# Linear-attention layer stack: queries held token by token, their denominators on VectorE, the FFN residual first on GpSimd

## The reference

```python
q = _phi((h @ wq + bq_).reshape(b, s, H, DH))        # _phi(t) = elu(t) + 1
k = _phi((h @ wk + bk_).reshape(b, s, H, DH))
v = (h @ wv + bv_).reshape(b, s, H, DH)
kv = jnp.einsum('bshd,bshm->bhdm', k, v)
z = 1.0 / (jnp.einsum('bshd,bhd->bsh', q, k.sum(axis=1)) + 1e-06)
att = jnp.einsum('bshd,bhdm,bsh->bshm', q, kv, z).reshape(b, s, d)
h = h + att @ wo + bo_
h = _ln(h, g1_, be1_)
y = jax.nn.gelu(h @ w1 + c1_, approximate=False) @ w2 + c2_
return (_ln(h + y, g2_, be2_), None)
```

## Time and profile before

| what | us |
| --- | --- |
| median of 3 runs | 918.11 (917.62 to 920.5) |
| the profiled execution | 918.29 |
| its span, first to last instruction | 916.2 |

### The profile page before, as it was taken

How to read it: one execution, slowest core, us unless ns; L and a number is a source line. 1 busy time by engine, 2 the same in 40 slices (tenths; PEclk the granted TensorE clock), 3 DMA queues, 4 the chain that set the end, 5 groups by cost and what they waited for, 6 DMA issues and landing times.

```text
span 916.2 us, 19024 instructions
## 1 busy us (share of the span) xinstructions
PE 877.0 (96%) x5786; PEld 746.0 (81%) x5786; DVE 765.4 (84%) x2737; ACT 705.5 (77%) x1104; POOL 241.2 (26%) x272
## 2 busy tenths in 40 slices
PE   6799999999999999999999999999999999998876
PEld 3588888888888888888888888888888888877664
DVE  7888789787987878788888878878897888899898
ACT  4799887878787887878787788878878787876553
POOL 5222221322232223312232233222223222212103
PEclk9999999999999999999999999999999999999895
DMA  4200100010000100010000100001000000000002
GB/s 130 73 1 17 26 1 22 1 42 1 0 21 0 40 1 20 0 40 0 1 21 0 40 1 19 2 16 25 1 21 0 0 0 1 9 17 1 1 1 92
DMA packets 21888, 16.21 MB, mean 18 GB/s; under 512 B 3920, under 2 KB 17855, under 8 KB 21824
## 3 DMA queue, kind: packets, MB, share of 16 engines
q1 hardware_dynamic: 20960, 14.95, 5.8%
q10 hardware_dynamic: 864, 0.59, 0.2%
HBM read 13.43 MB, written 2.10 MB: 17 GB/s over the span
## 4 chain that ended last, share of the span: by engine, by line
PE 78%; DVE 16%; issue 4%; ACT 1%; DMA 0%; DVEq 0%; ACTq 0%
PE down_ps L753 21%; PE q_ps L703 6%; PE small_ps L692 5%; PE q_ps L685 5%; PE att_ps L722 5%; PE k_ps L679 5%; PE up_ps L747 4%; PE up_ps L745 4%; PE up_ps L746 4%; PE t_ps L729 3%; PE t_ps L669 3%; DVE st L963 2%; PE small_ps L697 2%; PE att_ps L711 1%; PE small_ps L706 1%
## 5 line engine op out<-in xcount | busy, mean ns | idle before, releaser
L753 PEld LDWEIGHTS down_ps<-w_use,hid 128*128 128x128 f32 x2048 | 249.6, 192 | 29.3 <-issue 29.2
L753 PE MATMUL down_ps<-w_use,hid 128*128 128x128 f32 x2048 | 260.4, 275 | 0.0
L1004 POOL TENSOR_TENSOR res_att<-z_tm,g_att 128x512 f32<-128x512 f32 x64 | 81.5, 1273 | 495.9 <-DVE mv L969 495.9
L855 ACT ACTIVATE hid<-up_ps 128x512 f32<-128x512 f32 x192 | 114.9, 599 | 19.9 <-PE up_ps L747 4.3
L963 DVE BATCH_NORM_STATS2 st<-h 128x6 f32<-128x128 f32 x512 | 105.5, 279 | 2.3
L881 ACT ACTIVATE den<-q_ps,den_eps_col 128x512 f32<-128x512 f32 x64 | 43.9, 686 | 59.1 <-PE q_ps L703 59.0
L1011 POOL TENSOR_TENSOR res_ffn<-z_tm,g_ffn 128x512 f32<-128x512 f32 x64 | 81.5, 1273 | 20.7 <-DVE h L958 20.7
L938 ACT ACT_TABLE_LOAD x63 | 80.8, 1283 | 1.1
L745 PE MATMUL up_ps<-z_hi,w_hi 128*128 128x512 f32 x192 | 80.8, 421 | 0.4 <-DVE z_lo L998 0.4
L922 ACT ACT_TABLE_LOAD x62 | 79.5, 1283 | 1.1
L986 DVE TENSOR_SCALAR z_tm<-h,rstd,shift 128x128 f32<-128x128 f32 x256 | 76.3, 360 | 2.3
(11 more groups left out here) (200 smaller groups left out, 1780.1 us busy)
## 6 DMA issues: line engine op xcount, KB each, us to landing
raw_w<-in_L_attn_W SPq DMA_DIRECT2D x15, 256.0 KB, 4.8
out_y<-gate_tm SPq DMA_DIRECT2D x8, 256.0 KB, 2.1
bias_bc<-in_L_attn_c SPq DMA_DIRECT2D x7, 256.0 KB, 4.5
x_tm<-in_L_attn_x SPq DMA_DIRECT2D x3, 512.0 KB, 5.1
raw_g<-in_L_attn_g SPq DMA_DIRECT2D x14, 64.0 KB
x_tm<-in_L_attn_x SPq DMA_DIRECT2D x2, 256.0 KB, 3.2
raw_att<-in_L_attn_Wq SPq DMA_DIRECT2D x7, 64.0 KB, 1.8
raw_att<-in_L_attn_Wk SPq DMA_DIRECT2D x7, 64.0 KB, 1.9
```

The lines of the kernel that those rows point to most:

```text
L753: last = nc.tensor.matmul(down_ps[:, t, :], hid[:, j, t * P:(t + 1) * P], w2_use[:, j, :], start=False, stop=(j == FC - 1 and t == TT - 1))
L855: nc.scalar.activation(hid[:, j, :], up_bank[j], ACT.Gelu).then_inc(s["gelu"], 1)
L1004: nc.gpsimd.tensor_tensor(res_att[:, :, :], z_tm[:, b, :, :], g_att[:, :].unsqueeze(1).to_broadcast([P, TT, D]), ALU.mult).then_inc(s["t2m ...
```

## The change

Queries become token-major. `pe_q` issues four 128-column matmuls with the state as the stationary operand, where it issued one of 512 columns. `q_elu` (one VectorE instruction) takes the place of q_e's and q_phi's two, and leaves out the "+1", which is added where q_elu is read. The key sums now come out of L698's matmul equal on every partition (its operands are swapped), so that VectorE can multiply them with the queries (`dve_q_ks`), sum by head of 8 features (`dve_den`, 64 sums a partition), add the epsilon and take the reciprocal (`dve_rden`, two instructions of 64 elements), and divide (`dve_q_n`). The divided queries are transposed on TensorE (`pe_qn_transpose`, four transposes into the bank of `att_ps`) and copied to SBUF by ScalarE (`act_qn_copy`), and only then can the attention's bias matmul start its accumulation in that bank. `pe_den` and `act_den` are gone, and `blk` is masked for the key-value matrix alone (128 columns, not 256). The bias column that the keys' and queries' Relu read is gone too, with the GpSimd instruction that prepared the biases (L260), since "+1" is now in k_phi.

The order changes on every engine. TensorE: `pe_kz` stands after the second chunk of `pe_up`; `pe_q` follows `pe_k`; three chunks of `pe_down` are together; `pe_kvo` stands behind them; `pe_att` is last. ScalarE: the queries' Relu and Exp stand before `z1_hi`, `act_qn_copy` behind it. VectorE: h2's statistics are taken at the end of the period before; g_sb stands right behind h1; the W1 split and the zf tiles stand late. GpSimd: `res_ffn` comes first in a period, `res_att` after the layer's small instructions; `pool_vo` is parted into `pool_wv` and `pool_wo`, `pool_rows` into two parts in the fifth and sixth period of a layer.

The diff, cut to what the prediction speaks of (eight leading blanks and blank lines left out):

```diff
 def pe_q(pe, u, b):
     if after_first(u):
-        pe.wait_ge(s["den_sb"], u)
-    nc.tensor.matmul(q_ps[:, :], w_qk[:, 0:D], z_fm[:, b % 2, :], start=True, stop=True).then_inc(s["qproj"], 1)
+        pe.wait_ge(s["q_elu_s"], u)
+    for t in range(TT):
+        last = nc.tensor.matmul(q_ps[:, t, :], z_fm[:, b % 2, t * P:(t + 1) * P], w_qk[:, 0:D], start=True, stop=True)
+    last.then_inc(s["qproj"], 1)
...
 def pe_kv_ksum(pe, u):
     pe.wait_ge(s["g_sb_s"], u + 1)
+    if after_first(u):
+        pe.wait_ge(s["q_ks_s"], u)
     nc.tensor.matmul(KV_PS[:, 0, :], w_v[:, :], g_sb[:, :], start=True, stop=True)
-    nc.tensor.matmul(KV_PS[:, 1, :], g_sb[:, :], mean_f32[:, :], start=True, stop=True).then_inc(s["kv_ps_s"], 1)
-def pe_den(pe, u):
+    nc.tensor.matmul(KV_PS[:, 1, :], mean_f32[:, :], g_sb[:, :], start=True, stop=True).then_inc(s["kv_ps_s"], 1)
+def pe_kvo(pe, u):
     pe.wait_ge(s["blk_s"], u + 1)
-    pe.wait_ge(s["qphi"], u + 1)
-    nc.tensor.matmul(q_ps[:, :], blk[:, 1, :], q_phi[:, :], start=True, stop=True).then_inc(s["den_ps"], 1)
-def pe_kvo(pe, u):
-    nc.tensor.matmul(KVO_PS, blk[:, 0, :], w_o[:, :], start=True, stop=True).then_inc(s["kvo_ps_s"], 1)
+    nc.tensor.matmul(KVO_PS, blk[:, :], w_o[:, :], start=True, stop=True).then_inc(s["kvo_ps_s"], 1)
+def pe_qn_transpose(pe, u):
+    pe.wait_ge(s["qn"], u + 1)
+    if after_first(u):
+        pe.wait_ge(s["h1_s"], u)
+    for t in range(TT):
+        last = nc.tensor.transpose(att_flat[:, t * P:(t + 1) * P], q_nt[:, t, :], ident[:, :])
+    last.then_inc(s["qn_ps"], 1)
 def pe_att_bias(pe, u):
-    if after_first(u):
-        pe.wait_ge(s["h1_s"], u)
+    pe.wait_ge(s["qn_fm"], u + 1)
...
@@ -800,50 +815,55 @@
 def pe_period(pe, l, b, between=None):
     p, att, ln1, ffn, ln2, proj, state = stages(l, b)
+    keys = p + 1 if att else UNITS
     if ffn:
         if b == 2:
             pe.wait_ge(s["w1_split"], l * 2 + 2)
-        pe_up(pe, p - 2, p + 1 if att else UNITS)
+        pe_up(pe, p - 2, keys, (0, 1))
+    if att:
+        pe_kz(pe, p, b)
+    if ffn:
+        pe_up(pe, p - 2, keys, (2, 3))
+    read = pe_bank_job(pe, l, b, p)
+    if att:
+        if b == 0:
+            pe.wait_ge(s["wv_ready"], l + 1)
+        pe_kv_ksum(pe, p)
+    if ffn:
         if b == 2:
             pe.wait_ge(s["w2_ready"], l * 2 + 2)
         pe_down_bias(pe, p - 2)
+    if proj:
+        if b == SEQS - 1:
+            pe.wait_ge(s["qk_ready"], l + 2)
+        pe_k(pe, p + 1, b + 1)
+        pe_q(pe, p + 1, b + 1)
+    if between:
+        between()
+    if ffn:
+        pe_down(pe, p - 2, (0, 1, 2))
+    if att:
+        if b == 0:
+            pe.wait_ge(s["wo_ready"], l + 1)
+        pe_kvo(pe, p)
+    if ln1:
+        if read:
+            pe.wait_ge(*read)
+        pe_z1_transpose(pe, p - 1, p + 2 if state or not isinstance(p, int) else UNITS)
+    if att:
+        pe_qn_transpose(pe, p)
+    if ffn:
+        pe_down(pe, p - 2, (3,))
     if att:
         if b == 0:
             pe.wait_ge(s["ratt_ready"], l + 1)
         pe_att_bias(pe, p)
-        pe_kz(pe, p, b)
-    if proj:
-        if b == SEQS - 1:
-            pe.wait_ge(s["qk_ready"], l + 2)
-        pe_k(pe, p + 1, b + 1)
-    read = pe_bank_job(pe, l, b, p)
-    if att:
-        if b == 0:
-            pe.wait_ge(s["vo_ready"], l * 2 + 2)
-        pe_kv_ksum(pe, p)
-    if ffn:
-        pe_down(pe, p - 2, (0,))
-    if att:
-        pe_den(pe, p)
-        pe_kvo(pe, p)
-    if between:
-        between()
-    if ffn:
-        pe_down(pe, p - 2, (1,))
-    if ln1:
-        if read:
-            pe.wait_ge(*read)
-        pe_z1_transpose(pe, p - 1, p + 2 if state or not isinstance(p, int) else UNITS)
-    if proj:
-        pe_q(pe, p + 1, b + 1)
-    if ffn:
-        pe_down(pe, p - 2, (2, 3))
-    if att:
-        pe_att(pe, p)
     if state:
         if ln1:
             pe.wait_ge(s["z1lo_s"], p)
         pe_state_transpose(pe, p + 2, (b + 2) % SEQS)
+    if att:
+        pe_att(pe, p)
...
+def act_qn_copy(act, u):
+    act.wait_ge(s["qn_ps"], u + 1)
+    if after_first(u):
+        act.wait_ge(s["att_done"], u)
+    nc.scalar.activation(q_n[:, :], att_flat, ACT.Identity).then_inc(s["qn_fm"], 1)
 def act_z1_hi(act, u):
     act.wait_ge(s["t1_ps"], u + 1)
@@ -928,12 +944,12 @@
         act_zf_fm(act, l)
     if behind_keys:
         behind_keys()
-    if att:
-        act_den(act, p)
+    if proj:
+        act_q_exp(act, p + 1)
     if ln1:
         act_z1_hi(act, p - 1)
-    if proj:
-        act_q_exp(act, p + 1)
+    if att:
+        act_qn_copy(act, p)
     if is_unit(p - 1):
         nc.scalar.preload_act_table_set("gelu_and_others")
...
 def pool_period(pool, l, b):
     p = l * SEQS + b
     in_use = not isinstance(l, int) or l > 0
+    if is_unit(p - 2):
+        pool_res_ffn(pool, p - 2, (b - 2) % SEQS)
     if b == 0 and is_unit(p) and in_use:
+        pool_wo(pool, l)
         pool_row_att(pool, l, True)
+    if b == 1 and is_layer(l) and in_use:
+        pool_g_ffn(pool, l, True)
+        pool.wait_ge(s["gffn_ready"], l + 1)
     if b == 2 and is_unit(p) and in_use:
         pool_w2(pool, l, True)
+    if b == 4 and is_layer(l + 1):
+        pool_rows(pool, l + 1)
+    if b == 5 and is_layer(l + 1):
+        pool_row_parts(pool, l + 1)
     if b == 0 and is_unit(p):
         pool.wait_ge(s["gatt_ready"], l + 1)
     if is_unit(p):
         pool_res_att(pool, p, b)
-    if is_unit(p - 2):
-        pool_res_ffn(pool, p - 2, (b - 2) % SEQS)
-    if b == 1 and is_layer(l) and in_use:
-        pool_g_ffn(pool, l, True)
-        pool.wait_ge(s["gffn_ready"], l + 1)
-    if is_layer(l + 1):
-        if b == 3:
-            pool_bias(pool, l + 1)
-            pool.wait_ge(s["bias_s"], l + 1)
-            pool_rows(pool, l + 1)
-        if b == 6:
-            pool_qk(pool, l + 1)
-        if b == SEQS - 1:
-            pool_vo(pool, l + 1)
+    if b == 6 and is_layer(l + 1):
+        pool_qk(pool, l + 1)
+    if b == SEQS - 1 and is_layer(l + 1):
+        pool_wv(pool, l + 1)
 def dve_g_copy(dve, u):
...
 def dve_kvo(dve, u):
     dve.wait_ge(s["kvo_ps_s"], u + 1)
     nc.vector.tensor_copy(kvo[:, :], KVO_PS).then_inc(s["kvo_sb"], 1)
+def dve_q_ks(dve, u):
+    dve.wait_ge(s["kv_ps_s"], u + 1)
+    dve.wait_ge(s["q_elu_s"], u + 1)
+    if after_first(u):
+        dve.wait_ge(s["den_s"], u)
+    nc.vector.scalar_tensor_tensor(q_ks[:, :, :], q_elu[:, :, :], 1.0, KV_PS[:, 1:2, :].to_broadcast([P, TT, D]),
+                                   ALU.add, ALU.mult).then_inc(s["q_ks_s"], 1)
+def dve_den(dve, u):
+    dve.wait_ge(s["q_ks_s"], u + 1)
+    if after_first(u):
+        dve.wait_ge(s["den_e_s"], u)
+    nc.vector.tensor_reduce(den[:, :], q_ks[:, :, :].rearrange("p t (h d) -> p (t h) d", d=DH), AX.X,
+                            ALU.add).then_inc(s["den_s"], 1)
+def dve_rden(dve, u):
+    dve.wait_ge(s["den_s"], u + 1)
+    if after_first(u):
+        dve.wait_ge(s["rden_s"], u)
+    nc.vector.tensor_scalar(den_e[:, :], den[:, :], DEN_EPS, None, ALU.add).then_inc(s["den_e_s"], 1)
+    dve.wait_ge(s["den_e_s"], u + 1)
+    if after_first(u):
+        dve.wait_ge(s["qn"], u)
+    nc.vector.reciprocal(rden[:, :], den_e[:, :]).then_inc(s["rden_s"], 1)
 def dve_q_n(dve, u):
     dve.wait_ge(s["rden_s"], u + 1)
-    nc.vector.tensor_tensor(q_n[:, :], q_phi[:, :], rden[:, :], ALU.mult).then_inc(s["qn"], 1)
-def dve_k_phi(dve, u):
+    if after_first(u):
+        dve.wait_ge(s["qn_ps"], u)
+    heads = "p t (h d) -> p (t h) d"
+    nc.vector.scalar_tensor_tensor(q_nt[:, :, :].rearrange(heads, d=DH), q_elu[:, :, :].rearrange(heads, d=DH), 1.0,
+                                   rden[:, :].unsqueeze(2).to_broadcast([P, HT, DH]),
+                                   ALU.add, ALU.mult).then_inc(s["qn"], 1)
+def dve_k_floor(dve, u):
     dve.wait_ge(s["kexp"], u + 1)
     nc.vector.tensor_scalar(k_e[:, :, :], k_e[:, :, :], -1.0, 1.0, ALU.add, ALU.add).then_inc(s["tk"], 1)
+def dve_k_phi(dve, u):
     dve.wait_ge(s["tk"], u + 1)
-    nc.vector.tensor_tensor(k_phi[:, :, :], k_ps[:, :, :], k_e[:, :, :], ALU.max).then_inc(s["kphi"], 1)
-def dve_q_phi(dve, u):
+    if after_first(u):
+        dve.wait_ge(s["g_ps_s"], u)
+    nc.vector.scalar_tensor_tensor(k_phi[:, :, :], k_ps[:, :, :], 1.0, k_e[:, :, :],
+                                   ALU.add, ALU.max).then_inc(s["kphi"], 1)
+def dve_q_elu(dve, u):
     dve.wait_ge(s["qexp"], u + 1)
-    nc.vector.tensor_scalar(q_e[:, :], q_e[:, :], -1.0, 1.0, ALU.add, ALU.add).then_inc(s["tq"], 1)
-    dve.wait_ge(s["tq"], u + 1)
     if after_first(u):
         dve.wait_ge(s["qn"], u)
-    nc.vector.tensor_tensor(q_phi[:, :], q_ps[:, :], q_e[:, :], ALU.max).then_inc(s["qphi"], 1)
+    nc.vector.scalar_tensor_tensor(q_elu[:, :, :], q_e[:, :, :], -1.0, q_ps[:, :, :],
+                                   ALU.add, ALU.max).then_inc(s["q_elu_s"], 1)
...
@@ -1125,9 +1178,10 @@
         early()
     if ln1:
         dve_h1(dve, p - 1)
+    if att:
+        dve_g_copy(dve, p)
```

(49 more changed lines are left out.)

104 lines of the change are left out of this document (50 added, 54 removed).

## The result

The changed kernel takes 913.63 us (median) against 918.82 us for the kernel before in the same comparison: ratio 0.9935, 95% interval [0.9913, 0.9956]. The profiled execution has a span of 911.9 us (before 916.2) and an own time of 913.63 (before 918.29). Two of the five timed executions took 4868.20 and 4099.72 us; the ratio goes by the other three, 911.89, 913.39 and 913.63. The direction and the range of the prediction hold; its size does not: 5 to 6 us came where 12 were forecast.

A forecast was written before the change was run, and what follows sets the result against it. TensorE alone was taken to pace the middle: 0.28 us in each of 58 periods (-16.2), turns +1.4, splits +0.7, end +1.5, start +0.5, together -12.1, giving 906 us. The range was 896 to 920.

The forecast's parts named there:

- TensorE's pace, the main term: Middle periods: TensorE alone sets the pace, 0.28 us less in each of 58 periods, -16.2 us.
- The turns, "+0.2 for each": Periods behind the branch: TensorE waits 0.9 for g_sb against some 0.65 before, +0.2 in each of seven turns.
- The split: W1 split, now ahead of kvo: TensorE waits 0.7 us before pe_att, +0.1 a layer, from -0.6 to +0.3.
- "The end, +1.5": Last periods, paced by VectorE: 16.2 us each, +0.9 for three and +0.6 for the one before.
- one wait of 0.7: End periods: VectorE's new wait for z1_hi, 0.7 us, with no norms of h2 before z1_lo.
- The stretch behind the last attention: After the last g_sb: the prediction's sum had no term for it.
- First layer, +0.5 (from -1 to +2): Kernel's start: first three periods are latency chains of both kinds, +0.5 us, from -1 to +2.
- VectorE's new work: VectorE in each period: +1.1 us, to 11.2 of own work, with the reduce at 0.60 and reciprocal at 0.2.
- rival B: VectorE binds in some periods, two of eight by some 0.45: 7 us given back, 913 us; chance 0.16.
- GpSimd's order: res_ffn before res_att ends GpSimd's hold on VectorE: nothing where TensorE paced, up to 0.7 a period at the end.
- Rivals C: VectorE becomes the bound in every period through the chain from q_ks to q_n: 945 us, midway 930; chance 0.12.
- D: No gain: TensorE waits 0.4 for qn_copy because ScalarE is late, 921 us at most; chance 0.06.

The follow-up runs named there:

- tensor_more: Changed kernel with two more 128x128 fp32 matmuls (0.44 us of TensorE) in each looped period: 934.19 us, ratio 1.0165.
- affine_early: Changed kernel with VectorE's last affine (eight instructions) moved ahead of z1_lo in the last periods: 905.83 us, ratio 0.9866.
- fill_start: Changed kernel with 20 matmuls that nothing reads added ahead of the waiting transposes in periods 0 and 1: 908.05 us, ratio 0.9887.
- stats_first: Changed kernel with g_sb behind the statistics of h1 in periods 0 and 1, as in the kernel before: 911.68 us, ratio 0.9924.
- split_late: Changed kernel with the first W1 split moved in period 1 from ahead of the norms to behind z1_lo: 912.09 us, ratio 0.9936.
- no_reciprocal: Changed kernel with an ordinary min instruction of the same shape in place of the reciprocal: 910.16 us, ratio 0.9910.
- reduce_twice: Changed kernel with the head sum done twice in every period, the first into an unread tile: 929.69 us, ratio 1.0125.
- fill_end: Changed kernel with unread matmuls in the last four periods, five ahead of pe_kz and eight ahead of the key-value matmuls: 912.78 us, ratio 0.9942.

## Why the prediction was right and wrong

- **TensorE's pace, the main term: right.** 12.44 to 12.47 was forecast and 12.47 measured; tensor_more shows that it is TensorE's own work that counts. The middle lost 14.5 us for a forecast 11.7; a layer takes 103.08 us, 2.45 less than 105.53, of which eight times 0.28 are 2.24.
- **The turns, "+0.2 for each": failed, they cost nothing, and the reading under it was wrong.** I took the five waits for `g_sb` for waits at the turns. The timeline of the kernel before has them at 18, 809, 825, 841 and 857 us, at the start and the end; at the turns of the middle it lists none, before or after. VectorE's standstill behind the branch is shorter, 6.3 us over five turns, 1.26 each, where I had kept 1.94; it is hidden either way, and why it is shorter I did not try. The split cost a wait of 0.53 (3.7 / 7), for a forecast 0.7, and 0.59 before: slightly less, where I had +0.1. Over six layers these two terms are about 2.2 of the 2.8 us by which the middle did better than forecast.
- **"The end, +1.5": failed, it was over 5 us too little.** The prediction summed VectorE's instructions and one wait of 0.7 at full clock. VectorE's own work was right: 15.54, which affine_early lays bare, for 15.5. The wait was right too (0.78 with the clock held up), but the two together gave 16.60 and not 16.2. What it put at nothing, without a reason, is TensorE's clock: with VectorE as the pace TensorE waits 1.2 and 1.9 us in a row, and in two of the three periods the granted clock of what stands right behind fell, +1.1 in each, fed back through `z1_hi` into VectorE's chain. So 15.9 became 17.7. The three periods together grew by 4.0 us, for a forecast 0.9: 2.2 of the excess are the clock's.
- **The stretch behind the last attention: put at nothing, it cost 2.7.** From the last `g_sb` to the last instruction are 61.9 us, for 59.2 before; the sum has no term for it. In affine_early it is 60.8, so 1.6 us stay even without VectorE's wait. VectorE has the new work there too, but how the 1.6 come about stays open.
- **"First layer, +0.5 (from -1 to +2)": failed, by 3.5 to 5.5 us** (by the mark of the second table or of the first), and past its own range. The same cause: with the clock held up (fill_start) period 8 starts where it did before the change, within half a us of the forecast. The waits ahead of the falls are of the change (`q_nt` is on the path of the first attention, TensorE waits 1.64 for it, and then for the norms 3.50, behind q_ks, the reduce, the reciprocal and the split). What each instruction adds to these waits stays open; stats_first and split_late moved about 1 us each, hardly more than the spread of a profile.
- **VectorE's new work: +1.1 forecast.** Measured +0.93 busy a period, a figure that also holds what GpSimd's hold no longer adds. Of its parts the reduce took 0.68 in the timeline (I had 0.60, that is right for back-to-back work), `q_nt` 0.69 (right), the reciprocal 0.55 for 0.2. It cost nothing in the middle, as said (no_reciprocal); but the margin covered 0.34 a period on average, not 0.9 (reduce_twice), so rival B was closer than I had argued. The Trainium skill (VectorE: DVE Perf Modes, "First, the fixed hardware budget") has the reciprocal as an iterative divide with a repeat count of 8. The trace agrees that it is dearer than an ordinary instruction of its shape, by 0.36 us (553 and 195 ns), where my estimate from that page had 0.47 more.
- **GpSimd's order: right in the mechanism, half in size.** The hold on `m_r` went (0.82 to 0.15), which alone was worth 0.34 in two of the end periods, for 0.7, and nothing that the whole time shows.
- **Rivals C and D didn't come:** `q_nt` pays nothing for its repeated operand, and the wait for `qn_copy` is 0.12 of the 0.3 that would have cost the gain.

## What to carry to other kernels

A gain per period in a steady loop says nothing of the periods at either end: there the other engine paced, and what was put on it cost its own time and, where the waiting engine's clock fell for what came next, more than that. So write down for start and end which engine waits how long after the change, and look for work to put into a wait of the pacing engine first; a move of eight instructions past three others was worth at least as much as the whole change (7.8 us in the medians, for 5.2). Where nothing can be moved, a few matmuls that nothing reads can help, as at the start here; at the end they cost 1.4 us in one period and brought 1.1 in each of two (fill_end).

## What the chip showed that I had not expected

- TensorE's granted clock fell in stretches where the engine waited 1.2 to 3.5 us at a time (0.58 to 0.93 over 8 to 18 us), and four 128x128 fp32 matmuls took 1.91 right behind a wait of 1.90, for 1.06 at full clock: the slower of the two levels, 1.2 GHz. But the length of the waits doesn't settle it. The last end period has waits of 1.19 and 1.90 ahead of it in the changed kernel and of 1.19 and 1.89 in fill_start, and took 17.72 at 0.90 there and 16.60 at 1.00 here; reduce_twice has waits of 1.08 to 1.90 in its end periods and 1.00 in all three. What settles it no run here shows.
- A fall of the clock doesn't always cost. The kernel before made TensorE wait at its end too, two times a period, and kept 1.00 from 815 to 850; then its clock fell as well, for its last end period, which took the same 15.91 as the one ahead of it:

```profile
837.38 0.50 PE L716 MATMUL down_ps<-row_ffn,ones_r 128*128 128x512 f32 x1 [1.10 <-DVE h L958]
841.41 0.49 PE L697 MATMUL small_ps<-g_sb,w_v 128*128 128x128 f32 x2 [1.15 <-DVE g_sb L1042]
```

```profile
841.10:857.01 15.91, 13.31 (x76) 10.80 (x76) 14.86 (x59) 9.92 (x15) 2.49 (x3) 0.90 0.00 1
```

- Adding TensorE work shortened the kernel: 20 matmuls, 4.4 us of TensorE, brought 5.6 us in the medians (908.05 for 913.63), 4.4 by the ratios.
- A reciprocal of 128x64 fp32 takes 553 ns, a tensor_scalar of the same shape 195; a sum of 128x512 over groups of eight 684 ns in the timeline, 0.60 back to back, the same as a plain pass over 512 elements with one operand in PSUM (0.69 and 0.60).
